# Eight subtractions of a rounding step go from VectorE to GpSimd, and one pair of instructions changes places on VectorE

## The reference, cut to what matters

```python
# block 4
att = softmax(where(causal, -1e9, q @ k.T / 4));  x = x + (att @ v) @ w_out.T
# block 5: every one of four projections has an input scale of its own
ln_out = _ln(layernorm(x), ln_w, ln_b)
def _div_clamp_fp8(x, scale):
    y = clip(x / scale, -448, 448)
    y = y.astype(bfloat16).astype(float32)
    return y.astype(float8_e4m3fn).astype(float32)
q, qx, k, v = [_div_clamp_fp8(ln_out, s) * s @ w.T * w_scale for ...]
```

## Time and profile before

| what | before |
|---|---|
| median of three runs | 988.54 us |
| the profiled execution | 988.54 us |
| its span | 986.8 us |
| PE busy | 906.7 us (92%) |
| DVE busy | 708.0 us (72%) |
| ACT busy | 572.9 us (58%) |
| POOL busy | 134.3 us (14%) |

### The profile page before, as it was taken

One profiled execution on the slowest core, in us unless ns is written; L12 is line 12 of the kernel. 1 busy time (PEld: TensorE's weight loads), 2 busy tenths in 40 slices (PEclk: granted clock), 3 DMA queues, 4 the chain that ended last, 5 costly groups with the idle time before them and its releaser, 6 DMA issues.

```text
span 986.8 us, 15876 instructions
## 1 busy us (share of the span) xinstructions
PE 906.7 (92%) x5254; PEld 680.4 (69%) x5254; DVE 708.0 (72%) x1541; ACT 572.9 (58%) x2117; POOL 134.3 (14%) x186
## 2 busy tenths in 40 slices
PE   5989999999878699999999999999999997789796
PEld 3647566656667588888787878888787876555453
DVE  3673545555886887878788888878888888765653
ACT  3551334646747576877687777767786766331310
POOL 2001202000002121212112121212112121000000
PEclk9999999999999799999999999999999999889998
DMA  7001000000101223332332423423322622110000
GB/s 220 1 8 56 1 1 1 2 1 1 45 1 44 72 62 78 92 76 73 107 86 60 117 63 78 113 70 88 98 67 57 200 57 73 44 43 0 22 0 22
DMA packets 64083, 56.80 MB, mean 58 GB/s; under 512 B 11201, under 2 KB 62978, under 8 KB 64002
## 3 DMA queue, kind: packets, MB, share of 16 engines
q1 hardware_dynamic: 63904, 55.76, 21.0%
q10 hardware_dynamic: 98, 0.03, 0.0%
HBM read 21.15 MB, written 1.05 MB: 22 GB/s over the span
## 4 chain that ended last, share of the span: by engine, by line
PE 45%; DVE 23%; SPq 18%; DMA 4%; issue 4%; ACT 3%; POOL 1%; DVEq 0%; ACTq 0%
SPq L548 18%; PE ps L959 6%; DVE laid L1687 5%; PE ps L876 4%; DMA group_probsT<-laid 4%; PE ps L835 3%; PE ps L889 3%; DVE group_probs L1681 3%; PE ps L692 2%; PE ps L682 2%; PE ps L904 2%; PE ps L705 2%; PE ps L863 2%; PE ps L779 2%; PE ps L670 2%
## 5 line engine op out<-in xcount | busy, mean ns | idle before, releaser
L1261 ACT ACTIVATE group_probs<-ps,score_bias 128x256 f32<-128x256 f32 x256 | 117.2, 484 | 53.2 <-DVE score_bias L1670 53.2
L835 PE MATMUL ps<-group_w_hi,xq 128*128 128x256 f32 (+1 forms) x512 | 133.0, 301 | 0.2 <-DVE xq L1624 0.2
L1670 DVE TENSOR_REDUCE score_bias<-ps 128x2 f32<-128x512 f32 x128 | 88.0, 691 | 59.1 <-PE ps L889 59.1
L876 PE MATMUL ps<-group_probsT,group_values 128*128 128x512 f32 x256 | 120.2, 606 | 6.0 <-DVE x_all L1694 3.9
L835 PE MATMUL ps<-group_w_lo,xq 128*128 128x256 f32 (+1 forms) x512 | 122.7, 282 | 0.0
L1218 ACT ACTIVATE group_squares<-ps 128x128 f32<-128x128 f32 x384 | 108.6, 340 | 14.3 <-PE ps L835 10.8
L889 PE MATMUL ps<-group_kT,group_qT 128*128 128x256 f32 x512 | 116.5, 381 | 0.0
L889 PEld LDWEIGHTS ps<-group_kT,group_qT 128*128 128x128 f32 x512 | 97.7, 191 | 26.5 <-issue 9.6
L835 PEld LDWEIGHTS ps<-group_w_hi,xq 128*128 128x128 f32 x512 | 100.0, 195 | 1.5 <-issue 0.5
L835 PEld LDWEIGHTS ps<-group_w_lo,xq 128*128 128x128 f32 x512 | 99.9, 195 | 0.9
L1218 ACT ACTIVATION_READ_ACCUMULATOR group_squares<-ps 128x1 f32 x384 | 97.5, 273 | 0.0
(11 more groups left out here) (258 smaller groups left out, 1758.8 us busy)
## 6 DMA issues: line engine op xcount, KB each, us to landing
group_probsT<-laid SPq DMA_DIRECT2D x512, 64.0 KB, 2.0
group_raw_p<-in_L_xattn_wproj_dram SPq DMA_DIRECT2D x16, 256.0 KB, 3.4
group_raw_w<-in_L_xattn_wq_dram SPq DMA_DIRECT2D x8, 256.0 KB, 3.0
group_raw_w<-in_L_xattn_wqx_dram SPq DMA_DIRECT2D x8, 256.0 KB, 3.1
group_raw_w<-in_L_xattn_w_kv_x_dram SPq DMA_DIRECT2D x16, 128.0 KB, 3.3
x_all<-in_x_dram SPq DMA_DIRECT2D x2, 512.0 KB, 6.1
front_work<-in_ctx_dram SPq DMA_DIRECT2D x1, 1024.0 KB, 6.8
group_raw_w<-in_L_xattn_wk_dram SPq DMA_DIRECT2D x8, 128.0 KB, 3.3
```

The source lines that it names most:

```text
L835: last = pe.matmul(c.ps[:, bank, at:at + width], x_, w[:, k, col:col + width], start=k == 0 and m == 0, stop=k == KD - 1 and m == 1)
L876: last = pe.matmul(c.ps[:, bank, :].rearrange("p (i n) -> p i n", i=BLOCKS), c.values[:, item % 4, kt, side, :], c.probsT[item % 2][:, kt, ...
L1261: last = act.activation(c.probs[:, side, h, t, :], c.ps[:, fills.bank(name), t * S:(t + 1) * S], ACT.Exp, bias=c.score_bias[:, i:i + 1], a ...
L1670: v.tensor_reduce(c.score_bias[:, i:i + 2], c.ps[:, bank, :].rearrange("p (t n) -> p t n", n=S), AX.X, ALU.max, negate=True).then_inc(nega ...
```

## The change

The subtraction of `round_kind` leaves VectorE's list. VectorE signals a new semaphore `rounded` after its addition, and GpSimd does the subtraction in a new function `split`, with the same operands and the same output. GpSimd does all four of half 0 ahead of the first `head_scale`; those of half 1 stand between the `head_scale` of slots 1 to 3. Apart from this, `invert_heads(9)` and `take_heads(9)` of step 12 stand before the second layernorm of half 0, and no longer behind it.

```diff
-                    order.link(v.tensor_tensor(y, y, e, ALU.add))
-                    v.tensor_tensor(c.xq[:, KIND_ORDER[n], :, h, :], y.rearrange("p (k n) -> p k n", k=KD),
-                                    e.rearrange("p (k n) -> p k n", k=KD), ALU.subtract).then_inc(split_kind, 1)
+                    v.tensor_tensor(y, y, e, ALU.add).then_inc(rounded, 1)
...
-                        elif i % 2 == 0 and i < STEPS and i != OUT_STEP + 2:
+                        elif i % 2 == 0 and i < STEPS:
+                            if i == OUT_STEP + 2:
+                                invert_heads(i - 3)
                             take_heads(i - 3)
...
                     if i == OUT_STEP + 2:
                         normalise("Q2", 0, xn[0], twice[0], normed[0])
-                        invert_heads(i - 3)
-                        take_heads(i - 3)
...
+                def split(h, n):
+                    m = len(KINDS) * h + n
+                    pool.wait_ge(rounded, m + 1)
+                    y, e = y16[h][:, n % 2, :], e16[h][:, n % 2, :]
+                    pool.tensor_tensor(c.xq[:, KIND_ORDER[n], :, h, :], y.rearrange("p (k n) -> p k n", k=KD),
+                                       e.rearrange("p (k n) -> p k n", k=KD), ALU.subtract).then_inc(split_kind, 1)
...
                 root_of("Q2", 0)
+                for n in range(len(KINDS)):
+                    split(0, n)
                 head_scale(SLOTS[0], 0)
                 root_of("Q1", 1)
                 head_scale(SLOTS[0], 1)
                 root_of("Q2", 1)
                 head_scale(SLOTS[1], 0)
                 head_scale(SLOTS[1], 1)
+                split(1, 0)
                 head_scale(SLOTS[2], 0)
+                split(1, 1)
                 head_scale(SLOTS[2], 1)
+                split(1, 2)
                 head_scale(SLOTS[3], 0)
+                split(1, 3)
                 head_scale(SLOTS[3], 1)
```

More of the change, by code:

```diff
@@ L416, in front_stage @@
         lowered, averaged = st.sem("lowered"), st.sem("averaged")
-        scaled_kind, split_kind = st.sem("scaled_kind"), st.sem("split_kind")
+        scaled_kind, rounded, split_kind = st.sem("scaled_kind"), st.sem("rounded"), st.sem("split_kind")
         raw_loaded, late_loaded, hi_ready = st.sem("raw_loaded"), st.sem("late_loaded"), st.sem("hi_ready")
```

## The result

The changed kernel takes 994.27 us, the median of 8 runs (990.37 to 995.81), beside 988.68 us for the kernel before in the same session (8 runs). The ratio is 1.0052, with a 95% interval of 1.0028 to 1.0078. A second set of 12 runs gave 994.60 us (ratio 1.0041, 1.0010 to 1.0073). Each ratio in this document is to runs of the kernel before in the same session, whose medians went from 988.0 to 990.0 us. So the change makes the kernel some 4 to 5 us slower. The forecast was 990.8 us, its range 985.6 to 992.7: the side was the one that the forecast held likeliest, the size was too small, and the time lies outside the range.

What follows compares the result with a forecast made beforehand. VectorE was taken as the bound from step 12 to slot 0 and slot 1 to 3, then TensorE, later the transpose and DMA loop. 988.54 + 2.1 + 1.3 + 0.5 - 1.6 = 990.8 us, range 985.6 to 992.7.

Steps and rivals of the forecast that it cites:

- The moved pair, +2.1 by its order: Step 12, half 0: reciprocal and scaling ahead of the second layernorm lose their cover and delay every engine, +2.1 us.
- The clock at the moved layernorm, +1.3: TensorE's wait for the layernorm grows from 0.8 to 2.9 us, its clock falls, +1.3 us (between 0 and 1.5).
- the second rival: The clock does not fall at the moved layernorm: 989.5 us, chance 0.15.
- The subtraction on GpSimd, 2.25 us: Each subtraction moved to GpSimd takes 2.25 us there, bounds 1.2 and 3.0, against 1.225 us on VectorE.
- the fourth rival: GpSimd needs 3.0 us per subtraction, 0.75 more for each of three waited-for kinds: 992.9 us, chance 0.12.
- Taking turns: VectorE's SBUF instructions and GpSimd's subtractions exclude each other; three masks take 2 to 2.7 us instead of 0.43.
- The first rival: VectorE's tensor_scalars pass GpSimd freely, or VectorE keeps its turn through a whole rounding: 985.4 us, chance 0.17.
- Half 0, +0.5: Steps 13 to slot 0: held masks and TensorE's wait for the last subtraction make the second weight turn 0.5 us later.
- Half 1, -1.6: Slots 1 to 3: VectorE, freed of subtractions, lets ScalarE start 1.6 us earlier; bounds 0 and -3.4.
- the third rival: Slot 3's pauses shrink by 1.2 us and TensorE's clock stays up there: 988.7 us, chance 0.16.
- The last subtraction, 0.6 us on the block transpose, covered later: Half 1's kind 3 on GpSimd holds slot 3's last transpose, `laid` 0.6 us later; DMA-loop slack and TensorE's lead cover it.

Runs made afterwards that it cites:

- the pair alone: Kernel before with only the reciprocal and scaling of step 12 moved ahead of the layernorm, all subtractions on VectorE: 993.51 us, ratio 1.0062.
- one filler: The pair alone plus 20 overwritten transposes of a constant on TensorE in the pause before it turns the layernorm's result: 994.52 us, ratio 1.0051.
- two fillers: As with one filler, plus 12 more transposes ahead of the averaging of step 14: 994.35 us, ratio 1.0034; again 992.55 us, ratio 1.0057.
- half 1 only: Kernel before with only half 1's four subtractions on GpSimd, the last ahead of slot 3's scaling, pair not moved: 987.26 us, ratio 0.9978.
- delay only: Kernel before with the reciprocal done twice, ahead of the layernorm and again behind it, first result overwritten: 990.93 us, ratio 1.0028.

## Why the prediction was wrong, step by step

- **The moved pair, +2.1 by its order: right.** The layernorm starts 2.12 us late in every trace that has the pair, and with the clock kept up step 13 is 2.12 or 2.13 late.
- **The clock at the moved layernorm, +1.3: this is the step that failed.** That the clock would fall was right: it fell in all six traces with the pause of 2.9 us, so the second rival is out. The size was taken from a fall of 3 us; here the clock stayed low for 3 us in two traces and for 10 to 14 in four, and TensorE ran all the work in line behind the pause at the lower level. By the marks of the pair alone the loss beyond 2.1 us is 0.9 to 1.5 at step 13, 2.4 to 4.3 at the reciprocal ahead of slot 0, and 2.1 to 3.7 at slot 6; by the ratio of its times, about 4 (1.0062 x 988.5 less 988.5 is 6.1, less 2.1), with an interval of 2 to 6. Part of it is not this fall: with one filler there the clock fell after the pause ahead of the averaging of step 14, and another 1.5 us went. (The 0.8 and 1.1 us in the traces with two fillers are no such loss; by their rows they are mostly the second filler's own, which held the averaging.) I had priced the fall once and had the rest of the border shift rigidly behind it. That the clock at the layernorm costs the time up to step 13 is shown by three traces with a filler against six without; that keeping it up would give the median back is not shown, as all three sets with fillers stayed 3.4 to 5.6 us above the kernel before.
- **The subtraction on GpSimd, 2.25 us: right** (2.12 to 2.24), so the fourth rival, 3.0 us, is out. (Its sum should read 990.8 + 3 x 0.75 = 993.1, not 992.9.)
- **Taking turns: right in kind.** Three masks stand for 2.2 us, those that were named. The Trainium skill's rule ("SBUF — State Buffer", on the shared port pair) said that an instruction with one SBUF input in a 2-port mode would be held as well, and the trace agrees that such instructions stand: 2.23 us for a bf16 mask that takes 0.43 alone, and 3.0 for four scalings that take 1.14. The first rival, in which they pass freely, is out.
- **Half 0, +0.5: the wait was over-sized, and the net is not settled with the pair.** Without the pair the second turn of weights is 0.3 us early, not 0.5 late. TensorE waits 1.17 to 1.19 us for the last subtraction where 2 or more were forecast; the first turn is 1.2 late, and the idle time ahead of the second takes that up. In the changed kernel half 0 adds 0.2 to 0.3 us to the pair alone (first and third trace against the first of the pair), but the second traces of both differ by 1.9 the other way: there the clock fell again in the pair's (at 287.5) and not in the changed kernel's.
- **Half 1, -1.6: too small without the pair, not resolved with it.** From the reciprocal ahead of slot 0 to the low weight of slot 3 the three versions with all of half 1 on GpSimd and no pair gain 3.5, 3.3 and 2.8 us on the kernel before, about twice the forecast; in the first two the clock also stays up in slot 3, which was the third rival's condition. The changed kernel gains 2.2, 0.8 and 2.2 there, and the pair alone already 1.1 and 0.9, so between nothing and 1.3 is left for the subtractions; the clock fell in slot 3 as before (0.52 and 0.50 from 348 on). The shorter stretch between the low weights of slots 2 and 3 can't be used: the changed kernel gains 1.8 to 2.1 on the first trace of the kernel before, but so does the second trace of the kernel before (1.9).
- **The last subtraction, 0.6 us on the block transpose, covered later: wrong.** It holds the transpose for 1.9 us, and TensorE had no lead to cover it: the output products of slot 6 were late by the same 2.1 us until the subtraction was moved.

The ledger, as far as the runs carry it: the pair's loss beyond its 2.1 us is 2.1 to 3.7 by the marks of slot 6 and about 4 by the ratio, where the sum had 1.3, so 0.8 to 2.7 are missing; up to 2.1 come from the last subtraction. 990.8 and both are 991.6 to 995.6, with the measured medians (994.27 and 994.60) inside. How the excess divides between the clock and the last subtraction is known to 2 us only, since two traces of one kernel differ by as much, and the runs with fillers lose in the median what their traces don't show in the border. Why the low clock lasts 3 us in one execution and 14 in another with the same pause was not settled; that it goes with where step 10 began rests on six traces.

The forecast's sum also hid a choice. The two halves of the change have opposite signs: by the ratios the pair costs about 6 us (4 to 8) and the subtractions bring 2 to 3, with intervals that reach from none to 5. The versions without the pair are the ones to keep; which of them is best the times don't tell.

## What to carry to other kernels

Before an instruction is moved ahead of another, look who waits for that other one: the pair was free where it stood, inside a pause of its engine, and cost its whole 2.1 us where it was put, since TensorE's longest chain began at the layernorm. If the move also lengthens a pause of TensorE, don't price the low clock by the length of one other fall: here the same pause was followed by 3 to 14 us of it, so give it a wide range. And look at what else stands in the engine's path before a filler is put in: the second one here held up work that was ready. Work given from VectorE to GpSimd is worth only what VectorE's next instructions let it be: in these runs it cost nothing beside reads of PSUM, and less ahead of the scaling that GpSimd does for a slot than between its two tiles.

## What the runs showed of the hardware

- In 18 traces the same instruction, behind the same code, started at 245.2, about 248.2 or about 252.3 us, and medians of 8 to 35 runs of one kernel differed between sessions by 0.3 us (changed kernel) to 2.0 us (the kernel before).
- A pause of 2.9 us on TensorE was followed by 3 us at the lower clock in two traces and by 10 to 14 in four; one of 2.38 us was followed by none. The length of the pause alone does not decide: the 2.12 to 2.14 us ahead of the averaging of step 13 were followed by a fall in five traces (the kernel before twice, half 1 only, both with two fillers) and by none in three (one filler, delay only, the pair's second), and a pause of 2.67 us by a fall in two and by none in the changed kernel's second trace.
- Beside a GpSimd subtraction of 2.1 to 2.2 us, a VectorE mask on bf16 took 2.23 us instead of 0.43, four f32 scalings of 128 x 256 in SBUF 3.03 instead of 1.14, while four maxima out of PSUM took 2.48 us as they do alone:

```profile
344.21 2.48 DVE L1668 TENSOR_REDUCE score_bias<-ps 128x2 f32<-128x512 f32 x4
```
- GpSimd's subtraction (bf16 in, fp32r out, 128 x 1024) took 2.12 us beside instructions on PSUM and 2.24 where it met a mask; VectorE needs 1.225 us for it.
